# The first adapter's term of four up groups by four matmuls of 32 rows each, behind the four groups' other matmuls

## The reference

```python
def qat_lora_linear(x, W, b, A, B):
    Wq = fake_quant_weight(W)                       # rounded to 8 bits, times a scale
    base = jnp.einsum('bsi,oi->bso', x, Wq) + b
    lora = jnp.einsum('bsr,or->bso', jnp.einsum('bsi,ri->bsr', x, A), B)   # rank 16
    return base + SCALING * lora
h = qat_lora_linear(hidden_states, W_fc, b_fc, A_fc, B_fc)      # 1024 -> 4096
h = jax.nn.gelu(h, approximate=False)
h = qat_lora_linear(h, W_proj, b_proj, A_proj, B_proj)          # 4096 -> 1024
```

## Time and profile before

| | |
|---|---|
| time, median of 3 runs | 1079.26 us (1078.95 to 1079.86) |
| the profiled execution, slowest core | 1081.81 us |
| its span, first to last instruction (core 0) | 1080.3 us |
| spans of the eight cores | 1075.0 to 1080.3 us, granted clock 0.980 to 0.983 |
| TensorE busy | 979.4 us, 91% |
| ScalarE busy | 651.4 us, 60% |
| VectorE busy | 550.5 us, 51% |
| L690, the up groups' matmuls | 2048 of them, 261.5 us |
| L698, the adapter's matmuls | 256 of them |

### The profile page before, as it was taken

One profiled execution on the slowest core, in us unless ns is written; L12 is line 12 of the kernel. 1 busy time (PEld: TensorE's weight loads), 2 busy tenths in 40 slices (PEclk: granted clock), 3 DMA queues, 4 the chain that ended last, 5 costly groups with the idle time before them and its releaser, 6 DMA issues.

```text
span 1080.3 us, 23234 instructions; the slowest of 8 cores (1075.0 to 1080.3 us)
## 1 busy us (share of the span) xinstructions
PE 979.4 (91%) x8227; PEld 669.8 (62%) x8242; DVE 550.5 (51%) x1065; ACT 651.4 (60%) x948; POOL 59.8 (6%) x113
## 2 busy tenths in 40 slices
PE   4898888888898888998798899999999999999995
PEld 1343444444444444443356788888888888888884
DVE  4457787887878877689886502203031120402114
ACT  1346999999999999788552153444625445353541
POOL 4000111111111101100000000000000000000000
PEclk9998999999999999999899899999999999999998
DMA  9921334343554429879367300001000000100002
GB/s 131 168 86 45 106 121 115 111 128 99 147 141 131 130 71 269 211 206 271 116 191 226 112 1 16 25 2 40 2 26 16 16 26 1 41 1 21 21 12 69
DMA packets 35439, 99.05 MB, mean 92 GB/s; under 512 B 4544, under 2 KB 12992, under 8 KB 34944
## 3 DMA queue, kind: packets, MB, share of 16 engines
q0 software_dynamic: 15504, 52.96, 19.3%
q1 hardware_dynamic: 19824, 44.60, 13.6%
HBM read 97.54 MB, written 8.39 MB: 98 GB/s over the span
## 4 chain that ended last, share of the span: by engine, by line
PE 63%; DVE 12%; ACT 9%; issue 8%; DMA 7%; POOL 1%; DVEq 0%; ACTq 0%; SPq 0%; POOLq 0%
PE PSD L690 15%; PE PS L711 14%; PE PSD L540 8%; ACT PT L788 7%; PE PSD L711 5%; DMA WUK<-wUK 4%; PE PS L690 3%; DMA STG<-wPRr 3%; DVE QK L991 2%; PE PSD L552 2%; PE PSD L698 2%; PE PSD L648 2%; DVE XA L1046 2%; ACT RD L757 2%; PE BIG L571 2%
## 5 line engine op out<-in xcount | busy, mean ns | idle before, releaser
L788 ACT ACTIVATE PT<-PSD 128x1024 bf16<-128x1024 f32 (+1 forms) x288 | 271.2, 979 | 21.5 <-PE PSD L540 19.6
L690 PE MATMUL PSD<-XA,RTF 128*128 128x256 bf16 x1664 | 211.7, 275 | 3.9 <-ACT HH L837 2.8
L540 PE MATMUL PSD<-QK 96*64 96x512 bf16 (+7 forms) x1280 | 175.5, 356 | 33.5 <-ACT PT L788 19.0
L690 PEld LDWEIGHTS PSD<-XA,RTF 128*128 128x128 bf16 x1664 | 161.8, 99 | 26.7 <-issue 4.7
L711 PE MATMUL PS<-HH,RTP 128*128 128x256 bf16 x1536 | 177.3, 274 | 0.0
L837 ACT ACTIVATE HH<-PSD,BFCS,SML 128x256 bf16<-128x256 f32 x208 | 115.1, 565 | 79.7 <-PE PSD L698 79.2
L711 PEld LDWEIGHTS PS<-HH,RTP 128*128 128x128 bf16 x1536 | 150.2, 98 | 20.1 <-issue 1.7
L540 PEld LDWEIGHTS PSD<-QK 96*64 96x64 bf16 (+1 forms) x1280 | 63.4, 109 | 125.6 <-issue 115.0
L1009 DVE TENSOR_SCALAR PT<-PT 128x1024 bf16<-128x1024 bf16 (+3 forms) x288 | 108.2, 381 | 42.0 <-ACT PT L788 39.7
L1081 DVE TENSOR_SCALAR UPt<-PSD,SML 128x256 bf16<-128x256 f32 x8 | 3.9, 484 | 229.1 <-PE PSD L730 229.1
L1092 DVE TENSOR_TENSOR XA<-PTMP,XA 128x256 bf16<-128x256 f32 x64 | 27.2, 425 | 143.2 <-ACT PTMP L846 143.1
(11 more groups left out here) (188 smaller groups left out, 1203.2 us busy)
## 6 DMA issues: line engine op xcount, KB each, us to landing
STG<-wFCr POOLq DMA_DIRECT2D x32, 512.0 KB, 3.8
STG<-wPRr POOLq DMA_DIRECT2D x32, 512.0 KB, 3.9
STG<-wPRr SPq DMA_DIRECT2D x32, 512.0 KB, 4.4
STG<-wFCr SPq DMA_DIRECT2D x20, 512.0 KB, 4.6
XR<-xP POOLq DMA_DIRECT2D x16, 512.0 KB, 8.4
out<-OST SPq DMA_DIRECT2D x56, 128.0 KB, 2.0
QX<-wFCr SPq DMA_DIRECT2D x12, 512.0 KB, 5.5
XA<-xP POOLq DMA_DIRECT2D x3, 1024.0 KB, 33.7
```

The source lines that it names most:

```text
L540: mm = e.matmul(PSD[slot][64 * hf:64 * hf + 64, 512 * i + at:512 * i + at + ext], KH[c % 2][i][0:rows, 128 * kt + 64 * hf:128 * kt + 64 * ...
L690: e.matmul(UPB[oc % 5][:, 0:TC], RTF[:, 1024 * oc + 128 * i:1024 * oc + 128 * i + 128], xa(i, TC * t, TC), start=(i == 0), stop=False)
L788: e.activation(heads2(PTB[a % NPT], 0, ext), heads2(PSD[j % 2], 0, ext), AF.Exp, scale=ISQ).then_inc(s_exp, 1)
```

## The change

The ninth matmul of each up group is taken out. Behind the eight matmuls of every fourth group (`oc` = 3, 7, ..., 31) stand four matmuls in a row, one for each of the last four groups: 32 rows of `UO` at partitions 0, 32, 64 and 96, each into its own bank, each counting up `s_fc`. So the sums of four groups end together. This holds for all tiles, tile 0 too. The tiles `UZ`, their clearing and filling are gone; `factor` is one operation of 128 partitions for each `nb`.

```diff
@@ up(t, oc)
             if oc == 0:
-                e.wait_ge(s_uo, 5 + 4 * (t // 2) if t else 1)
+                e.wait_ge(s_uo, t // 2 + 1)
@@
-            q, r, o = oc // 4, oc % 4, TC * (t % 2)
-            if t:
-                lhs, rhs = BSF[:, 128 * q:128 * q + 128], UZ[r][:, o:o + TC]
-            else:
-                rows = slice(32 * r, 32 * r + 16)
-                lhs, rhs = BSF[rows, 128 * q:128 * q + 128], UO[rows, o:o + TC]
-            e.matmul(UPB[oc % 5][:, 0:TC], lhs, rhs, start=False, stop=True).then_inc(s_fc, 1)
+
+            if oc % 4 == 3:
+                o = TC * (t % 2)
+                for r in range(4):
+                    rows = slice(32 * r, 32 * r + 32)
+                    e.matmul(UPB[(oc - 3 + r) % 5][:, 0:TC], BSF[rows, 32 * oc - 96:32 * oc + 32],
+                             UO[rows, o:o + TC], start=False, stop=True).then_inc(s_fc, 1)
@@ factor(nb)
-            if nb == 0:
-                e.tensor_scalar(UO[:, :], BK[4][:, 0:512], SML[:, 1:2], None,
-                                ALU.mult).then_inc(s_uo, 1)
-            else:
-                for r in range(4):
-                    rows = slice(32 * r, 32 * r + 32)
-                    e.tensor_scalar(UZ[r][rows, :], BK[3][rows, 0:512], SML[rows, 1:2], None,
-                                    ALU.mult).then_inc(s_uo, 1)
+            e.tensor_scalar(UO[:, :], BK[4 if nb == 0 else 3][:, 0:512], SML[:, 1:2], None,
+                            ALU.mult).then_inc(s_uo, 1)
@@ dve, feed-forward loop
-                if dc == 5 and t == 0:
-                    for r in range(4):
-                        e.memset(UZ[r][:, :], 0.0).then_inc(s_uz, 1)
-                    e.wait_ge(s_uz, 4)
-                    for r in range(4):
-                        rows = slice(32 * r, 32 * r + 32)
-                        e.tensor_copy(UZ[r][rows, :], UO[rows, :]).then_inc(s_uo, 1)
```

More of the change, by code:

```diff
@@ L206, in build @@
     UO = at("UO", [128, 512], BF16, 175616)
-    UZ = [at("UZ%d" % r, [128, 512], BF16, 185856 + 1024 * r) for r in range(4)]
     HH = at("HH", [128, 32 * TC], BF16, 193024)
@@ L296, in build @@
     s_uo = sem("s_uo")
-    s_uz = sem("s_uz")
     s_fc = sem("s_fc")
```

## The result

The changed kernel takes 1094.24 us (median), the kernel before 1079.56 in the same comparison. The ratio is 1.0122, 95% interval 1.0108 to 1.0136, which is 13.2 us more (11.7 to 14.7). For each kernel one of four executions was far slower (1132.72 and 1205.51 us); the medians count it, the ratio does not. The medians are 14.7 us apart, which is the upper end of the ratio's interval. The prediction was 1095, in a range of 1086 to 1107. The profiled execution took 1093.66 us with a span of 1092.1 us on the slowest core, again core 0, 11.8 us over the span before.

What follows compares the result with a forecast made beforehand. TensorE was taken to bound tiles 1 to 7, VectorE's quantisation waiting for DMAs tile 0. Tiles 1 to 7 add 15.7 us, tile 0 and VectorE zero: 1079.3 + 15.7 = 1095 us, range 1086 to 1107 for eight in ten.

Steps and rivals of the forecast that it cites:

- The pack, distance p: Tiles 1 to 7: three further strips start p = 0.03 us apart; four groups take 3.90 us against 3.93.
- The round trip as a floor: Steady state: group 4q+5 may start 1.09 us behind the first strip, TensorE arrives at 1.17; free strips would hold 3.82.
- The end of the up groups: Ahead of the first down group: TensorE waits for Gelu 29, s0 (first strip's start) + 1.55 instead of 0.30, 1.25 us per tile.
- The table load: First pack, tiles 2 to 7: Gelu table loads behind the wait for the first strip; group 5 pauses 1.21 us.
- The start of a tile: Group 2 starts as before, behind the last tile's statistics; first strip of the first pack 4.08 us behind the tile's start.
- Sum of tiles 1 to 7: From tile start to first down group: +2.41 us each in tiles 2 to 7, +1.21 in tile 1, together +15.7.
- Tile 0: Down groups start 4.5 us earlier, but VectorE's DMA ring, without TensorE's work, sets the length: zero, gain at most 4.5.
- four signs that I had named for being wrong: Table load right behind the square, packs over 4.0 us apart, clock 0.50 behind a pause, tile 1 over 1 us earlier.
- The hoisted table load: Rival, chance 0.12: the load isn't behind the wait, tiles 2 to 7 lose as tile 1, 8.5 us, time 1088.
- strips without overlap: Rival, chance 0.10: the strips of a pack don't overlap, p = 0.109, +25.9 us, time 1105.
- the falling clock: Rival, chance 0.10: clock falls in TensorE's new pauses; 1117 if all 13 bring it, 1107 if only the seven at ends.
- gain through tile 0: Rival, chance 0.05: VectorE's ring follows TensorE, tile 0 gains up to 4.5 us; time 1078.5 or 1074 at its corners.

Runs made afterwards that it cites:

- The two timed kernels: The kernel before with the pack of four strips in tile 0 only, ratio 0.9989; the changed kernel with tile 0 as before, ratio 1.0134.

## Why the prediction was right, step by step

**The pack, distance p.** The term that was mis-sized: 0.03 us taken, 0.003 measured, worth 129 x 0.027 = 3.4 us in the sum. I had taken the row of two 64-column strips; the row of four 32-column strips in the earlier trace rows was near the right value. The Trainium skill ("TensorE: Matmul & The Clock Gate", Part 3) has about 4 ns, and this trace agrees with its 3 to 4. Row strips of 128 columns overlap as well as those column strips of 32. The price of going into strips and out is the one of tile 0 before: the next full matmul 0.22 behind the first strip, the first strip 0.10 late. The sum at p = 0 is 11.8 by its own terms, and 12.3 at 4 ns, not 11.9 and 12.4; nothing hangs on that.

**The round trip as a floor.** Right. By the matmuls alone a pack of four groups would take 3.808 + 0.012 = 3.82 us; it took 3.853, and group 5 followed group 4 after 0.92 instead of 0.87 us. The step said that a Gelu's start and its return hold the group at 3.82 if the strips are free. What it lacked is the 0.05 us of ScalarE's second wait: I had read the Gelu's start in tile 0, where there is none, and tiles 1 to 7 of the same trace already had 0.43. Without the second wait the pack took 3.820 us and group 5 followed after 0.88.

**The end of the up groups.** Right in mechanism, 1.42 instead of 1.25 us. TensorE goes on at s0 + 1.71 instead of 1.55: the Gelus start 0.44 behind the strip instead of 0.38 (the second wait again), and from the end of Gelu 29 (649.14) to the matmul it was 0.25 instead of 0.14. What makes these 0.11 wasn't tested; this matmul too has a second wait ahead of it.

**The table load.** Right: 1.15 instead of 1.21 us, in six tiles and not in tile 1. It rested on one row of a program's first load, and the experiment that loads the table early settled it.

**The start of a tile.** Right: group 2 starts at 684.78, which is 2.22 behind the tile's start (2.23 before), and s0 lies 4.06 behind it (4.08 predicted).

**Sum of tiles 1 to 7.** +15.7 predicted; the up parts give 1.04 + 6 x 2.36 = +15.2. The smaller p (3.4 us less) and the longer Gelu path (some 2.9 more) nearly cancelled, so that the sum is better than its terms, and that is luck: with the right p alone it would have been 12.3. The nearness of 1095 to the measured median has a part of luck too, since tile 0's gain of 1.2 wasn't in it either.

**Tile 0.** The step that failed, by a little in the whole time, though by more than I had allowed in the profile. The first half held: the first down group starts 39.16 us behind the tile's start instead of 43.80, 4.6 earlier where 4.5 was said. But I put what is left of that at zero, since the ring of DMA, rounding and freeing had none of TensorE's work in it. VectorE's wait of 1.78 us at 580.98 was in the list between two pieces of that ring, and it went:

```profile
578.52 0.47 DVE L1072 TENSOR_SCALAR UPt<-PSD,SML 128x256 bf16<-128x256 f32 x1
580.09 0.75 DVE L859 TENSOR_SCALAR STG<-STG,SML 128x1024 f32<-128x1024 f32 x1 [1.09 <-DMA STG<-wPRr]
```

The next piece is rounded at 580.09 instead of 581.38; 1.09 us of the gained time went into a wait for its DMA. The two timed kernels give 1.2 and 1.3 us for tile 0. In the slowest core's trace tile 1 starts at 616.65 instead of 620.03, 3.4 us earlier, and more than 1 us earlier was one of the four signs that I had named for being wrong. On that core the clock fell once behind a pause among the down groups of tile 0, for one down group of 5.92 us, instead of twice, for groups of 5.29 and 5.32:

```profile
593.04 5.92 PE L708 MATMUL PS<-HH,RTP 128*128 128x256 bf16 x32
594.00:595.00 1.00, 1.00 (x7) 0.67 (x6) 0.60 (x1) 0.00 (x0) 0.00 (x0) 0.50 0.92 356
```

Against 3.66 us at the full clock these groups are 2.3 and 1.6 + 1.7 us longer, so up to 1.0 us of the 3.4 may be the clock's. Whether tile 0 gains anything on a given core depends on that too, and I can't tell the two shares apart.

**The rivals.** The hoisted table load, strips without overlap and the falling clock are refuted by rows shown above. The one on the other side, gain through tile 0, was right in its first step and small.

## What to carry to other kernels

Matmuls put together behind several groups end those groups' sums together, so ask of every wait on them what it was hiding: here a function table that was loaded under the first group, and a bank that the next stage takes over from the last but two. Price the round trip TensorE, ScalarE, TensorE against the free banks; here it was the floor that a cheaper matmul did not get below. When such a change loses, the cover can be given back by an early dummy of the function and another order of banks, and then the change gains.

## What the runs showed of the hardware that I had not expected

- Row strips of 32 rows by 128 columns in the four row groups start 3 to 4 ns apart, each into its own bank (0.29 us for four of 0.278).
- A second semaphore wait ahead of an activation, though long met, delays its start by 0.05 us: 0.43 against 0.38 us behind the matmul; moving 31 of 32 of them away brought the packs from 3.853 to 3.82 us. In the chain that ended last the two waits stand as separate pieces of ScalarE's sequencer (L831 and L833, 0.02 us each).
- In profiles of one program tile 0 differed by up to 3.4 us (before) and 3.8 us (after) from core to core. In the kernel before the three cores on which the clock fell twice among the down groups took 87.1 to 87.8 us for it, the five others 84.4 to 86.8. A gain of 1.2 us there shows only in means.
